# Graph attention by group sums: another order on ScalarE and TensorE, the edge windows loaded by SyncE, the block sums stored by ScalarE

## The reference

```python
h = layer_norm(x, ln1_g, ln1_b)
qkv = (h @ Wqkv + bqkv).reshape(N, 3, H, DH)          # N = 625, H = 8, DH = 64
logits = jnp.einsum('ehd,ehd->eh', q[src], k[dst])    # 20,000 edges
a = logits + dist_attn + path_attn
e = jnp.exp(a - segment_max(a, dst)[dst])
sa = e / segment_sum(e, dst)[dst]
agg = segment_sum(v[src] * sa[:, :, None], dst)
```

## Time and profile before

| | |
|---|---|
| median of 3 runs | 859.73 us (856.99 to 859.93) |
| the profiled execution, its own time | 858.02 us |
| its span | 856.4 us |
| PE, DVE, ACT, POOL busy | 703.6, 524.8, 421.7, 162.2 us |
| attention stage, from the first issue to the last `collect` | 94.6 to 356.4 us |
| one of the short instructions of the stage: `collect` (DVE), mask (DVE), reciprocal (DVE), read of the total (DVE) | 0.28, 0.17, 0.16, 0.08 us |
| a copy of block sums on ACT; the issue of its store on SP | 0.695; 0.430 us (medians) |
| bytes moved by DMA | 125.63 MB |

### The profile page before, as it was taken

The page is one execution under the profiler, slowest core; times in us unless marked ns, Lnnn a source line. Parts: engine busy times, 40 slices in busy tenths (PEclk is TensorE's granted clock), DMA queues, the critical chain, the costliest instruction groups (busy, mean ns, idle before and its releaser), DMA issues. The chain is left out here.

```text
span 856.4 us, 14647 instructions
## 1 busy us (share of the span) xinstructions
PE 703.6 (82%) x4980; PEld 550.1 (64%) x4980; DVE 524.8 (61%) x1107; ACT 421.7 (49%) x689; POOL 162.2 (19%) x242
## 2 busy tenths in 40 slices
PE   3997506676666767599999999999999999999993
PEld 2663203354444444348988867987889899988782
DVE  6658415587677733264432265527888788888864
ACT  5235202466666644256444364215676666766740
POOL 7342425455445310000000000310000000000022
PEclk9999765599999965699999999999999999999998
DMA  8232774555666454250000204395677666777224
GB/s 273 64 58 33 181 117 132 174 158 160 174 158 172 155 187 158 59 200 1 1 1 1 74 3 146 122 340 192 216 240 234 219 216 237 256 234 236 88 58 142
DMA packets 104125, 125.63 MB, mean 147 GB/s; under 512 B 32370, under 2 KB 70028, under 8 KB 103532
## 3 DMA queue, kind: packets, MB, share of 16 engines
q1 hardware_dynamic: 96955, 115.06, 42.8%
q0 software_dynamic: 5600, 6.54, 3.4%
q10 hardware_dynamic: 1488, 3.01, 1.5%
HBM read 94.91 MB, written 29.67 MB: 145 GB/s over the span
## 5 line engine op out<-in xcount | busy, mean ns | idle before, releaser
L2128 PE MATMUL ps<-xT,w_hi 128*128 128x480 f32 (+7 forms) x512 | 110.1, 337 | 2.4 <-DVE hT L1947 2.2
L1021 PE MATMUL ps<-onehot,group_weights 128*32 128x314 bf16 x1272 | 63.1, 341 | 43.8 <-ACT sums_out L976 23.9
L919 DVE TENSOR_SCALAR onehot<-iota_h,windows 128x628 bf16<-128x628 f16 x212 | 75.0, 417 | 32.1 <-DMA windows<-window_scratch 16.6
L2128 PEld LDWEIGHTS ps<-xT,w_hi 128*128 128x128 f32 x512 | 82.0, 189 | 9.9 <-DVE hT L1947 4.1
L1021 PEld LDWEIGHTS ps<-onehot,group_weights 128*32 128x32 bf16 x1272 | 36.8, 110 | 69.4 <-issue 42.2
L1933 DVE TENSOR_TENSOR w_lo<-weights_far,w_hi 128x1024 fp32r<-128x1024 f32 x64 | 78.0, 1220 | 2.5 <-ACT w_hi L2043 2.2
L2130 PE MATMUL ps<-xT,w_lo 128*128 128x240 f32 (+7 forms) x512 | 74.5, 268 | 0.0
L2130 PEld LDWEIGHTS ps<-xT,w_lo 128*128 128x128 f32 x512 | 73.5, 190 | 1.5
L976 ACT ACTIVATE sums_out<-ps 128x628 f32<-128x628 f32 x53 | 36.8, 695 | 70.8 <-PE ps L1021 50.4
L940 DVE CUSTOM_DVE_ANT_0 weights<-sums_in,exponents 126x628 f32<-126x628 f32 x40 | 34.4, 861 | 57.3 <-issue 30.8
L2043 ACT ACTIVATE w_hi<-weights_far 128x1024 fp32r<-128x1024 f32 x64 | 67.2, 1052 | 0.0
(11 more groups left out here) (308 smaller groups left out, 1551.7 us busy)
## 6 DMA issues: line engine op xcount, KB each, us to landing
weights_far<-in_L_ffn_w SPq DMA_DIRECT2D x64, 512.0 KB, 5.9
sums_scratch<-sums_out SPq DMA_DIRECT2D x53, 314.0 KB
weights_near<-in_L_ffn_w SPq DMA_DIRECT2D x32, 512.0 KB, 3.6
sums_in<-sums_scratch SPq DMA_DIRECT2D x40, 309.1 KB
weights_near<-in_L_gnn_W SPq DMA_DIRECT2D x4, 1024.0 KB, 5.5
weights_near<-in_L_ffn_sw SPq DMA_DIRECT2D x8, 512.0 KB, 5.2
weights_near<-in_L_gnn_Wqkv SPq DMA_DIRECT2D x3, 1024.0 KB, 7.6
weights_ff<-in_L_gnn_W SPq DMA_DIRECT2D x1, 3072.0 KB, 14.2
```

The lines of the kernel that those rows point to most:

```text
L919: dve.tensor_scalar(onehot[w % 3][:, j, :], iota_h, windows[:, w % RING, j, 1:2], None, ALU.is_equal)\
L1021: last = pe.matmul(psW[r, a, :], R[w % 3][:, j, :, part], onehot[w % 3][:, j, a * SH:(a + 1) * SH], start=part == 0, stop=part == 2)
L2128: pe.matmul(both(bank, cap), w[u % 2][0][:, c, cut], xT(r)[:, c, :, :], start=c == 0, stop=False)
```

## The change

The change touches only the first part's end and the attention stage:

- ACT's order in a unit: before `keep(u-1)`, `exps(u)`, `norm(u)`; now `norm(u)`, `exps(u+1)`, `keep(u)`. PE's and DVE's orders follow; `logits` no longer waits for `collect`, since the output bank moves.
- The leading blocks use two pairs of PSUM banks in turn instead of one.
- SP loads the even windows below 16 and all from 16 on (`BOTH_QUEUES`); POOL loads only the odd ones below 16. ACT, not SP, issues the stores of the block sums.
- SP no longer waits for all rounds of records before window 6, only before window 20. Each queue loads two windows instead of three before the stage.
- Zeroing `rows_d` (3 MB) is issued by ACT in three pieces during `projections`, no longer in one piece at the start of the attention. Five small loads of vectors for the feed-forward layer go from SP's first place in the stage to its last.
- `low_part` of rounds 1 and 2 moves from POOL to DVE, with `values(2)` and `rest_part(1)` sooner on DVE and `powers(2)` sooner on ACT; one more filler matmul call (`keep_awake`).

```diff
@@ sync, attention
-        for i, vec in enumerate((bo, b2)):
-            sp.dma_start(rows_b[:, i * D:(i + 1) * D], ...)
...
         for r in range(1, len(ROUNDS)):
             store_parts(sp, r, rec2, rec2_d, lo_ready, windows_stored)
-        sp.wait_ge(windows_stored, 16 * len(ROUNDS))
...
+            def load(w):
+                if w < WB and (w % 2 == 0 or w >= BOTH_QUEUES):
+                    wait_past(sp, windows_stored, stored_for(w))
+                    window_free(sp, w)
+                    load_groups(nc, sp, mybir.EngineType.SP, w, tab, rec2_d, windows, g_in)
             def blocks(ws):
                 for w in ws:
-                    if w + AHEAD < WB and (w + AHEAD) % 2 == 0:
-                        window_free(sp, w + AHEAD)
-                        load_groups(nc, sp, mybir.EngineType.SP, w + AHEAD, tab, rec2_d, windows, g_in)
-                    sp.wait_ge(w_copied, w + 1)
-                    sp.dma_start(sums_d[w, :, :], sums_out[w % 3]).then_inc(out_done[w % 3], 16)
+                    load(w + AHEAD)
...
-            blocks(range(blocks_by(0)))
+            for w in range(LOADED, AHEAD):
+                load(w)
+            blocks(range(window_blocks(0) + 1))
             unit_rows(0)
             unit_rows(1)
+            blocks(range(window_blocks(0) + 1, leading))
@@ vector, attention
             for u in range(UNITS_ALL):
-                ws = list(unit_blocks(u + 1))
-                guards(u)
-                for w in ws[0:1]:
-                    group_weights(w)
-                if u % 2 and u >= 3:
-                    collect((u - 3) // 2)
-                weights(u)
-                for w in ws[1:]:
+                weights(u)
+                if u % 2 == 0 and u:
+                    collect(u // 2 - 1)
+                if u + 1 < UNITS_ALL:
+                    guards(u + 1)
+                for w in unit_blocks(u + 1):
                     group_weights(w)
@@ scalar, attention
-        act.dma_start(rows_d[0:SLOTS, :].rearrange("(a p) n -> p a n", p=DH),
-                      zeros[0:DH, :].unsqueeze(1).broadcast_to([DH, SLOTS // DH, D])).then_inc(rows_zeroed, 16)
...
+            def stored(w):
+                act.wait_ge(w_copied, w + 1)
+                act.dma_start(sums_d[w, :, :], sums_out[w % 3]).then_inc(out_done[w % 3], 16)
...
             for u in range(UNITS_ALL):
-                ws = list(unit_blocks(u))
-                for w in ws[0:1]:
-                    copied(w)
-                if u:
-                    keep(u - 1)
-                exps(u)
-                for w in ws[1:]:
-                    copied(w)
-                norm(u)
-            keep(UNITS_ALL - 1)
+                norm(u)
+                if u + 1 < UNITS_ALL:
+                    exps(u + 1)
+                keep(u)
+                for w in unit_blocks(u):
+                    copied(w)
+                    stored(w)
@@ tensor, attention
             for u in range(UNITS_ALL):
                 ws = list(unit_blocks(u))
-                if u % 2 == 0 and u:
-                    logits(u // 2)
-                if u % 2 and u >= 3:
-                    weighted_sums((u - 3) // 2)
                 for w in ws[0:1]:
                     sums(w)
-                if u:
-                    turn(u - 1)
+                if u % 2 and u + 1 < UNITS_ALL:
+                    logits((u + 1) // 2)
+                if u % 2 == 0 and u:
+                    weighted_sums(u // 2 - 1)
+                turn(u)
                 for w in ws[1:]:
                     sums(w)
```

More of the change, by code:

```diff
@@ L165, in load_groups @@
         frm = region[bass.ds(starts[j], P * REC2)] if k else region[0:P * REC2]
-        eng.dma_start(windows[:, w % RING, j, :], frm.rearrange("(p c) -> p c", p=P)).then_inc(g_in[w % RING], 16)
+        eng.dma_start(windows[:, w % RING, j, :], frm.rearrange("(p c) -> p c", p=P)).then_inc(g_in[w >= BOTH_QUEUES][w % RING], 16)
 def groups_in(w):
-    return 16 * sum(min(GW, GROUPS - GW * i) for i in range(w % RING, w + 1, RING))
+    first = BOTH_QUEUES if w >= BOTH_QUEUES else 0
+    return 16 * sum(min(GW, GROUPS - GW * i) for i in range(first + w % RING, w + 1, RING))
 def keep_awake(pe, bank, ident, filler, times):
@@ L250, in program @@
                     projections(nc, sem, src, dst, edge_attr_8, edge_attr_8_n2, x, Wqkv, bqkv, Wo, ln1_g, ln1_b,
-                                rec_d, rec2_d, y_d, wo, w_near, qT, kT, PT, rec, rec2, groups, windows, edge, upper, xs, hT, vs, work, small,
+                                rec_d, rec2_d, y_d, rows_d, wo, w_near, qT, kT, PT, rec, rec2, groups, windows, edge, upper, xs, hT, vs, work, small,
                                 tab_f, tab, iota_n, ident, ones, below, zeros, psum, banks)
@@ L349, in projections @@
          "seg_ends", "windows_stored", "gaps_zeroed"))
-    g_in = [sem(f"windows_in{i}") for i in range(RING)]
+    g_in = [[sem(f"windows_{when}{i}") for i in range(RING)] for when in ("in", "later")]
     flat = banks.rearrange("p a n -> p (a n)")
@@ L419, in _ @@
             sp.wait_ge(windows_stored, 16)
[L420 removed]
+            for w in range(0, LOADED, 2):
                 load_groups(nc, sp, mybir.EngineType.SP, w, tab, rec2_d, windows, g_in)
@@ L832, in halves, with psW, stored_for @@
         return tile.rearrange("p (a n) -> p a n", a=2)
+    leading = blocks_by(0)
+    def psW(w):
+        return banks[:, 6:8, 0:SH] if w < leading and w % 2 else banks[:, 4:6, 0:SH]
+    def stored_for(w):
+        return 16 * len(ROUNDS) if (w + 1) * GW > ROUND * GPB else 0
     def window_free(eng, w):
@@ L892, in _, with load @@
             pool.wait_ge(consts, 6)
+            def load(w):
+                if w < BOTH_QUEUES and w % 2:
+                    wait_past(pool, windows_stored, stored_for(w))
+                    window_free(pool, w)
+                    load_groups(nc, pool, mybir.EngineType.Pool, w, tab, rec2_d, windows, g_in)
+            for w in range(LOADED, AHEAD):
+                load(w)
             for w in range(WB):
-                if w + AHEAD < WB and (w + AHEAD) % 2:
-                    wait_past(pool, windows_stored, 16 * len(ROUNDS) if (w + AHEAD + 1) * GW > ROUND * GPB else 0)
-                    window_free(pool, w + AHEAD)
-                    load_groups(nc, pool, mybir.EngineType.Pool, w + AHEAD, tab, rec2_d, windows, g_in)
+                load(w + AHEAD)
                 pool.wait_ge(masked, w + 1)
@@ L1057, in _ @@
             logits(0)
-            for w in range(blocks_by(0)):
+            for w in range(leading):
                 sums(w)
```

97 lines of the change are left out of this document (58 added, 39 removed).

## The result

| | median, us | runs | ratio to before, 95% |
|---|---|---|---|
| before, beside the runs of after | 858.36 | 4 (855.25 to 859.93) | |
| after | 911.63 | 4 (910.17 to 912.86) | 1.0625 (1.0587 to 1.0663) |

The change makes the kernel slower by 53 us. The prediction, 852 (836 to 865), was wrong in sign and size. The profiled execution took 912.86 us, its span is 911.2.

A forecast was written before the change was run, and what follows sets the result against it. It took SP's instruction stream, 3.72 us per block, to bound the stage. Terms -1.0 - 8.1 + 1.5 = -7.6 took the profiled 858.02 to 850.4; the runs' median lies 1.7 above, so 852 us (836 to 865).

The forecast's parts named there:

- The start: Start of the attention stage: first unit rows asked for at 129 us (124 to 136) in place of 156.84.
- S: Time at which the attention stage starts: 91.8 us, between 91 and 95, in place of 94.58.
- The zeroing is hidden if the projections leave the DMA engines free: First part: early zeroing of `rows_d` delays the records by at most the few us by which S moves.
- The units up to 26: Attention units 0 to 26: SP's issues set 5.9 us per unit; `weights(26)` starts at 286.1, 1.0 before now.
- The bound by SP: Attention stage: SP's instruction stream is the bound, one block's loads costing it 3.72 us with nothing overlapping.
- The exponentials one unit ahead bring nothing here.: Units up to 26: computing `exps` one unit ahead gains nothing, since the unit's rows are what is late.
- The rival of the low clock: PE waits for SP and its clock stays low in the units: 31 us more, 883; chance 0.20 for 862 and more.
- The store on ACT: Units up to 26: ACT issuing block-sum stores costs nothing; without the cover 0.43 x 1.3 = 0.6 us per unit.
- Units from 26 on: Attention units 26 to 39: the new order takes 54.5 us in place of 62.6, 8.1 gained.
- The five vectors: End of the stage: feed-forward vector loads fit into about 18 us with about 2 to spare; otherwise up to 3 cost.

The follow-up runs named there:

- e11: e7 with the zeroing of `rows_d` issued in three pieces in units 27, 30 and 33 instead of the first part: 824.92 us.
- e10: The changed kernel with three unread filler matmuls of 192 columns on TensorE behind each unit's `turn`: 859.08 us.
- e16: The changed kernel with e10's filler matmuls and GpSimd loading the odd windows throughout: 864.52 us.
- e1: The changed kernel with the kernel before's order of the unit loops on VectorE, ScalarE and TensorE: 873.71 us.
- e2: The changed kernel with TensorE's `logits` and `weighted_sums` ahead of the block's `sums` in each unit: 860.65 us.
- e4: The changed kernel with the old unit order of e1 and GpSimd loading the odd windows throughout: 859.68 us.
- e7: The changed kernel with TensorE's matmuls reordered as in e2 and GpSimd loading the odd windows throughout: 820.30 us.
- e12: e7 with the block sums stored by SyncE as before, not by ScalarE: 827.68 us.
- e8: e4 with the block sums stored by SyncE as before, not by ScalarE: 842.77 us.
- e3: The changed kernel with GpSimd loading the odd windows through the whole stage as before: 916.82 us.
- e15: e7 run again, unchanged, beside the kernel with filler matmuls on the same chip: 822.66 us.
- e9: The changed kernel with ScalarE's copy and store of the unit's first block ahead of the next exponentials and `keep`: 873.80 us.

## Why the prediction was wrong, step by step

- **The start.** Right in what it removed. The idle stretch is gone, SP's block costs 3.70 us (3.72 worked out), the first unit rows are asked for at 134.86 (129, 124 to 136). S was put at 91.8 and is 96.25, above its range: "The zeroing is hidden if the projections leave the DMA engines free" failed. It slowed the loads of records by 3.3 us; without it S is 92.45 (e11).
- **The units up to 26: the step that failed.** "DVE's work fits below it: ... 4.0. ACT's too ... 3.8." These are sums of busy times, engine by engine. They say that no engine is full; they say nothing on the way around through the three. The same prediction did walk such a way, `logits`, `guards`, `exps`, for the units without blocks, and there it is right: the last pairs after take 402.84 - 395.96 = 6.88 us (7.2 worked out). It was never walked with a block in it. From the rows of before, at the full clock, the branch through ACT would have been copy 0.70, `sums` (at least 0.99 by e10's rows), `weighted_sums` 1.30 or `logits` 1.33, `collect` 0.28 every second time, `guards` 0.81, `exps` 0.78, `keep` 0.70: 5.56 or 5.31 with no gap, and 0.3 x 1.7 for the second block that 3 of 10 units have, 5.95 on average. That is already no less than the 5.9 of SP's stream. The branch through POOL has one-hots, mask and product in place of `exps`, `keep` and copy: 1.26 + 0.17 + 0.72 = 2.15 by the rows of before against 2.18, so the same. But the product takes 1.17 beside `weights`, where the new order puts it: 0.4 more in the units with one block, 6.2 on average. Measured: 6.26 (e16). At the low clock, with 1.76, 2.36 and 1.92 in it, the sum by ACT is 7.39 or 6.67 and 0.3 x 2.46, on average 7.77, and up to 0.3 more by POOL; measured 7.8.
- **The bound by SP** exists, but lay hidden under the circle: it shows in e1 and e2 at 6.2 us a unit, and is worth 14 us (e1 against e4) to 40 us (e2 against e7).
- **"The exponentials one unit ahead bring nothing here."** Where SP's stream is the bound, as the prediction had it, this holds: the old order (e1) and the opened new one (e2) take 6.26 and 6.21 us a unit. With SP's stream out of the way the new order as a whole gains: e12 runs 15 us below e8, from which it differs by the order of the units alone. To unit 26 it gains 0.23 us a unit, 6 us; the larger part, 17 us in the profiled executions, lies behind unit 26, where the prediction had counted on it. The two don't add up to 15, since e12's profiled execution took 4 us more after the attention. What the exponentials' place gives by itself no run tells.
- **The rival of the low clock** (0.20) named the right sign and the right reading, the clock well below 1.00 from 170 to 280 us; its price was 31 us, measured 52 (e3 against e16). Its cause, PE waiting for SP, was wrong: PE waited for ACT and POOL. It is as much a part of the miss as the circle: with the clock brought back and the circle left closed, e16 is at 864.5 and e10 at 859.1, inside the range of 836 to 865. The two lengthen each other: opening the circle brings the clock back (e2 0.87, e7 1.00), and bringing the clock back shortens the circle (e10).
- **The store on ACT "costs nothing; without the cover it is 0.6 per unit".** Both halves hold: nothing in the new order (e12), 17 us in the old (e4, e8), against 0.6 x 26 = 16.
- **Units from 26 on.** 8.1 us were to be gained; it is 63.1 us after in place of 62.6, because up to unit 29 blocks are still made and the circle turns: `weights(30)` starts at 373.25, 29.7 us for four units. The other nine took 33.4, 3.7 each, less than the 4.1 worked out. In e7, e12 and e15 this stretch took 47.5 to 51.5, better than the 54.5 worked out.
- **The five vectors** are hidden as said: POOL's additions end at 410.3, `collect` at 413.8.

The Trainium skill (TensorE: Matmul & The Clock Gate, section on loop structure) draws the loop in which VectorE's copy out of PSUM doesn't break the matmuls' clock as one whose next matmuls follow at once. Where they instead wait for that copy, as here, the row says otherwise: PE was busy for 66% and was granted 0.68.

What stays open: what decided between 1.00 in the kernel before and 0.68 after. The like busy shares, 65 and 66%, don't say that PE had like work: at the lower clock a matmul is counted as busy for longer (24 of `sums` 1.76 us in place of 0.99), and from 215 to 255 us it ran 273 of them in place of 396. Fewer matmuls and longer waits came together, and no run varied one of them alone.

## What to carry to other kernels

When instructions change places in several in-order streams, don't add each engine's work; start at one instruction, go to whatever must end before it, by data or by the stream it stands in, and see how long it takes to come back to it one unit later. Do it for every branch: here the one through ScalarE and the one through GpSimd were within 0.5 us of each other in the unit shown, so that opening one alone (e9) left the other. Put what another engine waits for ahead of bulk work in each stream: here two calls moved by two lines were worth 51 us. Test a low clock with matmuls placed where TensorE waits anyway; placed in the circle they hide their own gain. And take a bound away only to look for the next: the order alone gave back 51 us, the second queue 40 more, and the pair beats the kernel before by 38 us, which neither did alone.

## What the runs showed of the hardware

- TensorE, busy for 64 to 66% of a stretch with many waits of 0.5 to 2.8 us, was granted 0.67 to 0.71 of its clock in the three windows shown, and 0.91 to 1.00 from 135 us on with three more matmuls of 192 columns per unit (1.1 us, e10).
- GpSimd's product for a block took 1.17 us or more where it overlapped VectorE's `weights` (27 times from 140 to 350 us in the trace of after, as at 256.40), and 0.74 in the other 8. In e7 it was 1.17 in 21 such places and 0.68 to 0.74 in the other 17, with a median of 0.685.
- 3 MB of zeroing, issued in three pieces by ScalarE, lengthened 21 loads on another queue from 22.9 (e11) to 26.1 us (e7).
